# Attention and a mixture of experts on eight cores: matmuls as wide as each expert's list of rows, chosen by branches on TensorE, and a quarter of W2 of six experts rounded ahead of time

## What is computed

```
# layer: x = LN(x + attention(x)); x = LN(x + moe(x)).  D = 1024
q, k, v = x @ w_q, x @ w_k, x @ w_v          # 16 heads of 64, a window of 7 tokens around each
x1 = layernorm(x + softmax(q k / 8) v @ w_o)
top_w, top_i = top_k(x1 @ gate_w, 2)         # 2 of 8 experts for each token
top_w = softmax(top_w)
for e in range(8):                           # H = 4096
    h = relu(x1 @ w1[e] + b1[e]); y = h @ w2[e] + b2[e]
    out += comb[:, e] * y                    # comb is top_w where e is chosen, else 0
x = layernorm(x1 + out)
```

## Time and profile before

| | |
|---|---|
| median of 3 runs | 1559.03 us (1555.95 to 1567.98) |
| the profiled execution | 1563.76 us; span of its slowest core, core 1: 1562.1 us |
| the other cores' spans | 1525.3 to 1559.2 us |
| core 1, attention until the first matmul of `up` | 507.1 us |
| core 1, PE busy | 1371.2 us, 88% |
| core 1, DVE, ACT, POOL busy | 416.8, 443.9, 201.3 us |

### The profile page before, as it was taken

One profiled execution on the slowest core, in us unless ns is written; L12 is line 12 of the kernel. 1 busy time (PEld: TensorE's weight loads), 2 busy tenths in 40 slices (PEclk: granted clock), 3 DMA queues, 4 the chain that ended last, 5 costly groups with the idle time before them and its releaser, 6 DMA issues.

```text
span 1562.1 us, 25128 instructions; the slowest of 8 cores (1525.3 to 1562.1 us)
## 1 busy us (share of the span) xinstructions
PE 1371.2 (88%) x10374; PEld 829.9 (53%) x10374; DVE 416.8 (27%) x848; ACT 443.9 (28%) x703; POOL 201.3 (13%) x220
## 2 busy tenths in 40 slices
PE   3869887676761999999999999999999999999995
PEld 2434443343431764674575476467457547646742
DVE  1046454354563113112210310311221031031112
ACT  1314343343431321331231142133123114213311
POOL 3000000202022200210120030020012012002000
PEclk9989999898875999999999999999999999999998
DMA  9961632225674999999799899979979989997800
GB/s 168 187 135 26 203 94 82 96 82 106 164 195 153 182 194 165 204 193 169 167 194 169 167 191 171 190 148 198 165 170 192 166 173 190 168 185 121 168 27 31
DMA packets 112104, 240.09 MB, mean 154 GB/s; under 512 B 12104, under 2 KB 17608, under 8 KB 111984
## 3 DMA queue, kind: packets, MB, share of 16 engines
q0 software_dynamic: 88704, 189.07, 68.6%
q1 hardware_dynamic: 23280, 49.35, 10.2%
HBM read 335.80 MB, written 53.76 MB: 249 GB/s over the span
## 4 chain that ended last, share of the span: by engine, by line
PE 81%; issue 5%; ACT 5%; DVE 4%; DMA 2%; another core or an unknown queue 1%; POOL 1%; DVEq 0%; ACTq 0%; SPq 0%; POOLq 0%
PE m_pY L369 32%; PE m_pH L337 32%; PE a_pj L728 5%; PE a_pj L752 5%; PE a_pj L921 2%; DMA s_wA<-wq 1%; PE m_pH L313 1%; DVE a_sm L803 1%; ACT m_hT L347 1%; ACT a_x1T L975 1%; ACT a_pb L797 1%; PE a_tr L812 1%; PE a_pS L772 1%; PE a_pj L884 1%
## 5 line engine op out<-in xcount | busy, mean ns | idle before, releaser
L337 PE MATMUL m_pH<-m_xgT,s_wA 128*128 128x288 bf16 x4096 | 507.1, 287 | 8.0 <-ACT m_hT L347 7.2
L369 PE MATMUL m_pY<-m_w2b,m_hT 128*128 128x512 bf16 (+1 forms) x2560 | 503.4, 379 | 10.3 <-ACT m_hT L347 10.3
L337 PEld LDWEIGHTS m_pH<-m_xgT,s_wA 128*128 128x128 bf16 x4096 | 399.8, 98 | 115.9 <-issue 14.8
L369 PEld LDWEIGHTS m_pY<-m_w2b,m_hT 128*128 128x128 bf16 (+1 forms) x2560 | 227.2, 100 | 272.8 <-issue 13.0
L347 ACT ACTIVATE m_hT<-m_pH,s_b1pc 128x576 bf16<-128x576 f32 x256 | 189.1, 740 | 349.4 <-PE m_pH L337 341.2
L266 DVE SCALAR_TENSOR_TENSOR m_z<-m_pY,m_dec,m_z 128x1024 f32<-128x1024 f32 (+1 forms) x40 | 47.1, 1177 | 562.4 <-PE m_pY L369 512.9
L728 PE MATMUL a_pj<-a_xT,s_wA 128*128 128x470 bf16 (+1 forms) x640 | 122.9, 347 | 15.0 <-DMA s_wA<-wq 6.5
L291 ACT ACTIVATE m_fst<-m_fst,s_consts 128x1 f32<-128x1 f32 x40 | 11.7, 293 | 420.7 <-DVE m_fst L273 416.5
L256 DVE SCALAR_TENSOR_TENSOR m_z<-m_b2f,m_dec,m_z 128x1024 f32<-128x1024 f32 (+1 forms) x48 | 52.3, 1104 | 253.2 <-DMA m_z<-out,m_rix 252.7
L245 POOL DMA_INDIRECT out<-m_z,m_rix x40 | 40.1, 1003 | 603.5 <-ACT m_z L295 502.3
L728 PEld LDWEIGHTS a_pj<-a_xT,s_wA 128*128 128x128 bf16 x640 | 60.8, 100 | 72.8 <-issue 24.2
(11 more groups left out here) (137 smaller groups left out, 729.5 us busy)
## 6 DMA issues: line engine op xcount, KB each, us to landing
s_wA<-w POOLq DMA_DIRECT2D x32, 2048.0 KB, 54.9
m_w2b<-w POOLq DMA_DIRECT2D x32, 2048.0 KB, 27.3
xg<-a_zz SPq DMA_DIRECT2D x8, 1170.0 KB, 8.6
a_xr<-xh SPq DMA_DIRECT2D x16, 512.0 KB, 4.7
x1d<-a_xr SPq DMA_DIRECT2D x16, 512.0 KB, 2.8
out<-a_xr SPq DMA_DIRECT2D x16, 512.0 KB, 3.7
m_xgs<-xg SPq DMA_DIRECT2D x8, 1024.0 KB
m_b2f<-b SPq DMA_DIRECT2D x8, 512.0 KB, 10.0
```

The source lines that it names most:

```text
L337: lambda e, k=k, n=n: e.matmul(pH[b][:, n * 512: n * 512 + HC], w1b[g][:, k * GCOLS + (j % 8) * 128: k * GCOLS + (j % 8) * 128 + 128], xgT ...
L369: lambda e, out=out, lhs=lhs, fs=fs, j=j, g=g: e.matmul(out, lhs, w2b[g][:, (j % 8) * D + fs * 512: (j % 8) * D + fs * 512 + 512], start=( ...
```

## The change

**On PE.** `counts()` loads the 8 counts into registers of PE, before the first transposes. The whole list of an expert on PE, from `up(e, 0)` to `down(e, 4)` with the next expert's transposes between, is written three times, for 576, 544 and 512 columns, one after the other, and branches choose: over 544 rows the first, over 512 the second, else the third. In the second and third the second half of `up` has 256 or 224 columns in place of 288. In the third the short tile is left out, but for 4 matmuls of 64x64 that carry its semaphore counts. ACT's relu, DVE and POOL do the same work for all three widths; columns that are not written hold what stood in PSUM, which DVE clears once at the start.

**On DMA.** `cast_w2` issues, in attention's steps 0 to 11, 12 DMAs on POOL's queue that read 2 MB of W2 each, round it and write 1 MB to the new HBM tensor `wc`: quarter 3 of experts 1 to 6. The load of these quarters is then a plain copy of 2 MB on SP's queue.

```diff
+WIDTHS = (576, 544, 512)
+    def choose(self, eng, engobj, f, i):
+
+        was = dict(self.waited[eng])
+        if i + 1 == len(f.cols):
+            f.mode["cols"] = f.cols[i]
+            self.emit(eng, engobj, f.ops)
+            return
+        with engobj.If(f.count[0] > f.cols[i + 1]):
+            f.mode["cols"] = f.cols[i]
+            self.emit(eng, engobj, f.ops)
+        self.waited[eng] = was
+        with engobj.Else():
+            self.choose(eng, engobj, f, i + 1)
...
     def load_w2(e_i, g):
+        if (e_i, g) in v["cast"]:
+            w2_ev[(e_i, g)] = p.op(
+                "sp",
+                lambda e: e.dma_start(
+                    w2b[g][:].rearrange("p (c n) -> p c n", c=8),
+                    v["wc_d"].ap()[v["cast"][(e_i, g)]].rearrange("(c p) n -> p c n", p=128)),
+                waits=[("sPC", p.v["sPC"]), y_ev.get((e_i - 1, TT, g))], inc="sWC", k=16)
+            return
...
-                        pH[b][:, n * 512: n * 512 + HC],
+                        pH[b][:, n * 512: n * 512 + (HC if n == 0 else mode["cols"] - HC)],
...
+                def fn(e, out=out, lhs=lhs, fs=fs, j=j, g=g):
+                    n, full = 512, t < TT or mode["cols"] > TT * 128
+                    if not full:
+                        if fs == 0 or j % 8 != 7:
+                            return None
+                        n = REM
...
+        p.q["pe"][first:] = [(Choice(rows_of[e_i], WIDTHS, p.q["pe"][first:], mode), (), None, 1)]
...
+        if u < 12:
+            cast_w2(1 + u // 2, 3, u % 2)
```

More of the change, by code:

```diff
@@ L40, with __init__ @@
             "sW1_0", "sW1_1", "sW1_2", "sW1_3", "sW2_0", "sW2_1", "sW2_2", "sW2_3",
[1 row of a table removed]
[1 row of a table added]
             "sRC", "sXL0", "sXL1", "sGA0", "sGA1", "sGB0", "sGB1",
             "sO0", "sO1")
+class Choice:
+    def __init__(self, count, cols, ops, mode):
+        self.count, self.cols, self.ops, self.mode = count, cols, ops, mode
 class Prog:
@@ L86, in emit @@
         for fn, waits, incname, k in ops:
+            if isinstance(fn, Choice):
+                self.choose(eng, engobj, fn, 0)
+                continue
             for (sn, val) in waits:
@@ L140, in emit_experts, with counts, fn @@
     done = v["done"]
+    mode = {"cols": CAP}
+    rows_of = [[] for _ in range(NE)]
+    def counts():
+        def fn(e):
+            for i in range(NE):
+                rows_of[i].append(nc.values_load(
+                    v["cnts"][0:1, i:i + 1], engines=[mybir.EngineType.PE], min_val=0, max_val=ROWS,
+                    skip_runtime_bounds_check_because="a count of at most ROWS tokens"))
+        p.op("pe", fn, waits=[v["cnt_ev"][0]])
     def col(e_i, i, t, r0=0, r1=128):
@@ L299, in gather_T @@
         bank = pH[tt % 2][:].bitcast(BF16)
-        wt = [xg_ev[e_i], xt_ev.get((e_i, tt - 2))] + (done if e_i == 0 else [])
+        wt = [xg_ev[e_i], xt_ev.get((e_i, tt - 2))] + (done + [clear_ev] if e_i == 0 else [])
         if tt < 2:
@@ L337, in up @@
                     lambda e, k=k, n=n: e.matmul(
-                        pH[b][:, n * 512: n * 512 + HC],
+                        pH[b][:, n * 512: n * 512 + (HC if n == 0 else mode["cols"] - HC)],
                         w1b[g][:, k * GCOLS + (j % 8) * 128: k * GCOLS + (j % 8) * 128 + 128],
-                        xgT[:, k * CAP + n * HC: k * CAP + n * HC + HC],
+                        xgT[:, k * CAP + n * HC: k * CAP + (HC if n == 0 else mode["cols"])],
                         start=(k == 0), stop=(k == 7)),
@@ L366, in down @@
                     lhs = hT[:, j * CAP + t * 128: j * CAP + t * 128 + REM]
-                last = p.op(
[L368 to L372, removed]
+                def fn(e, out=out, lhs=lhs, fs=fs, j=j, g=g):
[4 more added lines that the diff above has]
+                        n = REM
+                    return e.matmul(
+                        out[:, 0:n], lhs, w2b[g][:, (j % 8) * D + fs * 512: (j % 8) * D + fs * 512 + n],
+                        start=(j == 0 or not full), stop=(j == 31 or not full))
+                last = p.op(
+                    "pe", fn,
                     waits=w if fs == 0 else (),
@@ L376, in down @@
                 y_ev[(e_i, t, g)] = last
+    counts()
+    for i in range(2):
+        clear_ev = p.op("dve", lambda e, i=i: e.memset(pH[i][:, 512:512 + HC], 0.0), waits=done, inc="sDVE")
     load_xg(0)
@@ L394, in emit_experts @@
             load_rec(e_i + 1)
+        first = len(p.q["pe"])
         for j in range(32):
@@ L1084, in counts @@
                  waits=[ev, self.rt_ev], inc="sDVE")
-        p.op("dve", lambda e: e.tensor_copy(cnts[:, 0:8], self.rw[:, 0:8]), waits=[f], inc="sDVE")
+        self.v["cnt_ev"].append(p.op(
+            "dve", lambda e: e.tensor_copy(cnts[:, 0:8], self.rw[:, 0:8]), waits=[f], inc="sDVE"))
         c = p.op("dve", lambda e: e.reduce_max(self.rs[:, 0:1], self.rw[:, 0:8], axis=AX.X),
@@ L1102, in emit_attention, with cast_w2 @@
                    waits=[v["ev_setup"]], inc="sDVE")
+    def cast_w2(e_i, g, h):
+        i = v["cast"].setdefault((e_i, g), len(v["cast"]))
+        r0 = h * GCOLS // 2
+        p.op("pool", lambda e: e.dma_start(
+            v["wc_d"].ap()[i, r0:r0 + GCOLS // 2, :],
+            v["w2_d"].ap()[e_i, g * GCOLS + r0:g * GCOLS + r0 + GCOLS // 2, :]), inc="sPC", k=16)
     a.rt_ev = None
@@ L1276, in build_nc @@
     yg_d = nc.dram_tensor("yg", [XROWS, D], F32)
+    wc_d = nc.dram_tensor("wc", [6, GCOLS, D], BF16)
     x1_d = nc.dram_tensor("x1d", [CORE_T, D], F32)
@@ L1289, in build_nc @@
         cnts = sbp("cnts", [128, 16], I32)
+        cnt_ev = []
         scr = sbp("scr", [128, 16], F32)
         eps, neg, tokf, half = consts[:, 0:1], consts[:, 1:2], consts[:, 24:40], consts[:, 40:41]
-        w_ev, w1_ev, done = {}, {}, []
+        w_ev, w1_ev, cast, done = {}, {}, {}, []
         with ExitStack() as SW:
```

## The result

The kernel became **slower: 1617.18 us** (1612.64 to 1628.35, 4 runs) against 1563.51 us of before in the same comparison, a ratio of 1.0367 (95% interval 1.0256 to 1.0479). Now and then one half of the chip runs an execution of any of these kernels at a lower clock; the medians here are of all executions (before has 1559.03 us without such a one), while ratios, and the medians of single cores, leave these out. Forecast were 1570 us and a range up to 1597. The profiled execution's slowest core is core 1 again, with a span of 1612.4 us where before had 1562.1: +50.3 us, where the sum had +11.3.

The account below looks back on a forecast made before the run. PE's stream was taken to bound the eight experts. On core 1, -34.0 (`up`), -6.6 (short tiles) and +51.9 (branches) gave +11.3 us: 1575.1 us profiled, 1570 us as median, range 1536 to 1597.

Parts of the forecast that it names:

- the sum: All terms for core 1: -34.0 in `up`, -6.6 for short tiles, +51.9 for branches, together +11.3 us.
- What bounds the kernel: In the eight experts PE's stream is the bound, about 129 us each; the weight queue runs dry around an expert's end.
- The lists: Widths each core takes, worked out from the routing: on core 1 six experts of 544 columns and two of 512.
- Gain in `up`: Narrower matmuls in the second half of `up`, at 0.415 ns per column: -34.0 us on core 1.
- The floor of 101 ns: Possible least time of a narrow matmul in `up`, from attention's matmuls; would give back 2.6 us per 512-column expert.
- Gain in the short tile: Leaving it out between two experts saves 3.3 us, PE starting 4.4 us after tile 3; -6.6 us on core 1.
- The cost of a jump: Each long jump of PE over an expert's list taken as 4.45 us; branches together +51.9 us on core 1.
- The bound from above: Upper limit for one jump of PE: 7 us, from 4.5 us of PE's row and 2.5 us for full queues.
- rival D: Jumps between experts cost 6 us or more, fetching through full queues: median 1592 us at 6 us, 1612 at 7; chance 0.25.
- The clock's term: PE's clock at half speed after idling: 2 us added to each gap of over 4.5 us between experts.
- The start of the experts: Before expert 0, one jump with 3.4 us of cover from PE's wait for the copies: +1.0 us.
- The other edits: Register loads (3.9 us), clearing of `pH` and casts in attention are hidden, cost nothing; casts at worst up to +10 us.

Follow-up runs that it names:

- widths_fixed: Changed kernel without branches, core 1's widths written into the program for every core, casts kept: 1530.69 us, ratio 0.9795 to the kernel before.
- branches_alone: Changed kernel with its branches and three lists, but all lists at 576 columns with the full short tile, no casts: 1675.89 us, ratio 1.0702.
- branches_by_eight: Changed kernel with a branch around every eight columns of `up` and one around the short tile, in place of whole experts, no casts: 1838.37 and 1833.04 us.
- near_branches: Changed kernel with a branch around every two columns of `up` and one around the short tile, in place of whole experts, no casts: 1704.76 us, ratio 1.086.
- short_jump: Changed kernel with 576 columns everywhere, one branch per expert around the short tile alone, no casts: 1576.69 us; repeated, 1577.82 us, ratio 0.9974.

## Why the prediction was wrong

The forecast had the direction (over 1% slower stood at 0.40), but not the size: the sum had +11.3 us, and +50.3 came. The steps in turn:

- **What bounds the kernel** held. PE's stream sets the end: in widths_fixed narrower matmuls alone made the kernel 2% faster. The loads were nearer than the sum had them, by the 5.6 us of waiting for W2 there, but the long gaps of the change cover this.
- **The lists** held. Core 1's transitions have the numbers of branch records that 544, 512, 544, 544, 544, 512, 544, 544 give.
- **Gain in `up`** held. In the chain, 320 matmuls of a 512 list took 35.11 us and 336 of a 544 list 39.09 us: 109.7 and 116.3 ns on average, where the line of the earlier trace rows gives 109.6 and 116.3. The floor of 101 ns from the earlier trace rows isn't there. The chain, core 1:

```profile
681.51 35.11 PE m_pH L381 x320
...
1492.42 39.09 PE m_pH L381 x336
```

- **Gain in the short tile** held: `up` of expert 2 starts 3.56 us behind the four small matmuls that are left, 4.5 us behind tile 3's end, with DVE's copies as the releaser (the sum had 4.4).
- **The cost of a jump failed**, by the step "I take 4.45 us, PE's own row". That row was a jump over idle queues. The bound from above, 7 us, was too low as well: the second and third jumps took up to 9.6 us. In the sum the gaps between experts were 2 x 10.85 + 3 x 6.4 = 40.9 us. Measured they are 19.2 and 17.2 (544 to 512) and 13.0, 12.0 and 7.3 (544 to 544; 13.0 with the 1.8 us just behind it), together 68.7 us. The argument held against rival D, "the share has its dip there", is true of the first jump only, and the two behind it meet the loads that are issued at this very point. Rival D named this mechanism and had 0.25. The 13 jumps that the sum leaves uncovered took 6.4 us on average. D's own figure for 6 us, 1592, leaves out the 2 us of clock that the prediction's rule adds behind each of the two 512 lists, and its 1612 for 7 us has them; with them 6 us give 1596.
- **The clock's term failed** too. I charged 2 us to five gaps. All seven gaps between experts, also the two of 3.6 us behind a 512 list, were followed by matmuls at a granted clock of 0.50; the first 64 of an expert took 9.5 to 10.8 us where 7.0 to 7.4 us would be full speed. That is 20 us in place of 10. The window behind such a short gap:

```profile
779.00:782.00 3.00, 2.96 (x14) 1.95 (x15) 2.35 (x10) 1.62 (x3) 0.41 (x1) 0.50 1.01 225
```

- **The start of the experts**: 510.02 us against 507.07, so +3.0 where I had +1.0. That it isn't more is luck. PE stood 7.25 us before `up` where it had stood 0.78, so the jump of 7.1 us added 6.5; the 3.4 us of cover were not there, because the sequencer reached the branch at 502.4 us, 0.4 us before the last transpose ended. The transposes themselves had begun 3.5 us earlier than before (498.46 against 501.98 us); why stays open.
- **The other edits** held: register loads, the clearing of `pH` and the casts are hidden. Two softmax sums of attention in the chain still lie 20.36 us apart, as in the earlier trace rows, now at a DMA share of 1.00 where up to 0.9 was forecast:

```profile
173.82 1.23 DVE a_sm L859
...
194.18 1.23 DVE a_sm L859
...
180.00:200.00 20.00, 16.43 (x178) 8.59 (x177) 9.60 (x14) 9.09 (x15) 1.47 (x2) 1.00 1.00 191
```

The sum with these sizes, in the prediction's order: -34.0 for `up`; -13.4 for two short tiles less the small matmuls that stay, and +7.1 for the waits on DVE in their place; +3.0 at the start; +68.7 for the gaps; +20 for the clock. That makes +51.4 us; the spans differ by 50.3. Against the forecast the gaps are 27.8 us of the difference, the clock 10 and the start 2.

The Trainium skill (Runtime: NRT & Kernel Launch, Instruction fetch mechanics) says that a taken branch outside the prefetched pages makes the sequencer fetch by DMA first. The long records agree: each has one or two blocks of instructions inside it. The Trainium skill (Advanced Engine Details and Errata, Control Flow Timing) has a compare-and-branch at about 108 ns. The 0.08 us of a branch that isn't taken and the 0.2 to 0.37 us of a short jump are of that order, the 3.3 to 9.6 us of a long one are not.

Open: the last 5 us by which widths_fixed and branches_alone overshoot the change on core 1, and whether the casts add anything beside the branches (1.0249 and 1.0367, with intervals that overlap). That branches_by_eight is slower than both finer and coarser ones fits its records: it decides anew 24 times inside `up`, each time at the price of a long jump, where the change never does and near_branches mostly pays 0.2 us, though the two fetch about the same (125 and 127 blocks from 500 us on). It wasn't run with idle queues. The exact distance at which a jump becomes long was not measured: 128 instructions were short in short_jump, some 256 took anything from 0.2 to 8.4 us in branches_by_eight, and the lists of some 830 matmuls were long.

## What to carry to other kernels

A branch on PE costs by whether its target is near or far (not by how far) and by what the DMA queues hold: a duration read where the queues were idle is the lower bound, not the value, and the point where a branch stands often is the point where the next loads are issued. Decide once per kernel with a long jump, use short jumps only alone, and keep them out of a dense stream while weights are loaded. Where the time is that of the slowest core, look first which core that is on the chip at hand, and whether the change reaches it. When a stage loses its tail (here the short tile), ask what then ends the wait and whether the clock falls in it.

## What the runs showed of the hardware that was not expected

- A taken long jump on PE: 3.5 to 5.6 us with idle queues, 6.0 to 9.6 us behind loads of weights, with its first block of instructions starting 0.6 to 1.5 us and 1.9 to 5.6 us after the jump (second and third jumps of a transition); a jump over 128 instructions 0.37 us at most when alone.
- 366 branches in a stream cost core 1 115.3 us of "issue" with the DMA share at 1.05 to 1.08 in the windows shown, and 12.7 us without the loads behind expert 0, of which 12.3 in expert 0 itself.
- A gap of 3.6 us was enough for the granted clock to read 0.50 in the 3 us behind it, for a loss of 2.7 and 3.1 us (10.15 and 10.49 us for 64 matmuls against 7.4). The same gap cost some 1.5 us in widths_fixed.
